# First attention of a two-layer model: own values of four heads in one group of matmuls, every second round

## The reference

```python
x = x + _L0_attn_ref(_L0_cond_ref(x, ...), ...)
x = x + _L0_ffn_ref(_L0_cond2_ref(x, ...), ...)
x = x + _L1_attn_ref(_L1_cond_ref(x, ...), ...)
x = x + _L1_ffn_ref(_L1_cond2_ref(x, ...), ...)
```

```python
def _cross_head_proj(inputs, qw1, qw2, kw1, kw2, qdd, kdd):
    h_q = jnp.einsum('bnts,btin->btsi', inputs, qw1)
    out = inputs + jnp.einsum('btsi,btin->bnts', h_q, qw2)
    h_k = jnp.einsum('bnts,bsin->btsi', inputs, kw1)
    out = out + jnp.einsum('btsi,bsin->bnts', h_k, kw2)
    out = out + inputs * jnp.transpose(qdd, (0, 2, 1))[:, :, :, None]
    out = out + inputs * jnp.transpose(kdd, (0, 2, 1))[:, :, None, :]
    return out
...
logits = _cross_head_proj(logits, pre_qw1, pre_qw2, pre_kw1, pre_kw2, pre_qdd, pre_kdd)
mask = jnp.tril(jnp.ones((t, t), dtype=bool))
logits = jnp.where(mask, logits, jnp.finfo(jnp.float32).min)
probs = jax.nn.softmax(logits, axis=-1)
probs = _cross_head_proj(probs, post_qw1, post_qw2, post_kw1, post_kw2, post_qdd, post_kdd)
o = jnp.einsum('bnts,bnsh->bnth', probs, v)
```

## Time and profile before

| | |
|---|---|
| median of three runs | 1061.58 us |
| the profiled execution's own time | 1062.01 us |
| its span, first to last instruction | 1060.2 us |
| mean granted TensorE clock | 0.942 |
| TensorE busy | 929.1 us (88%), 6216 matmuls |
| VectorE busy | 791.1 us (75%) |
| ScalarE busy | 575.2 us (54%) |
| GpSimd busy | 187.5 us (18%) |
| chain that ended last | PE 57%, DVE 25%, DMA 6% |

### The profile page before, as it was taken

The page is one execution under the profiler, slowest core; times in us unless marked ns, Lnnn a source line. Parts: engine busy times, 40 slices in busy tenths (PEclk is TensorE's granted clock), DMA queues, the critical chain, the costliest instruction groups (busy, mean ns, idle before and its releaser), DMA issues.

```text
span 1060.2 us, 18270 instructions
## 1 busy us (share of the span) xinstructions
PE 929.1 (88%) x6216; PEld 662.9 (63%) x6216; DVE 791.1 (75%) x2089; ACT 575.2 (54%) x1458; POOL 187.5 (18%) x168
## 2 busy tenths in 40 slices
PE   2889998999899989789999999788898998899993
PEld 2777776777677767664576666623333337788883
DVE  7579988998899889985299997567666766366664
ACT  2689568956795679541143332136474761455551
POOL 1101030103010301027434433200000005011111
PEclk9989998999899989969999999969998987799997
DMA  9999940000000000034367774515464544788773
GB/s 251 201 209 252 245 101 1 2 1 2 1 1 1 2 1 1 1 112 167 121 217 247 232 228 133 209 53 184 161 236 161 193 168 139 268 324 306 274 269 130
DMA packets 71453, 153.81 MB, mean 145 GB/s; under 512 B 11439, under 2 KB 53054, under 8 KB 67136
## 3 DMA queue, kind: packets, MB, share of 16 engines
q1 hardware_dynamic: 65696, 139.93, 43.5%
q0 software_dynamic: 5664, 12.71, 3.3%
HBM read 122.09 MB, written 62.19 MB: 174 GB/s over the span
## 4 chain that ended last, share of the span: by engine, by line
PE 57%; DVE 25%; DMA 6%; issue 5%; ACT 4%; POOL 3%; SPq 1%; DVEq 0%; POOLq 0%; ACTq 0%
PE ps L1785 53%; DVE arena L1191 2%; DVE arena L1535 2%; DVE den L1033 2%; DMA arena<-slots 2%; DMA arena<-split 2%; DVE arena L1174 2%; DMA made<-arena 2%; POOL slots L580 1%; POOL arena L542 1%; DVE arena L1764 1%; DVE den L986 1%; DVE arena L1217 1%; DVE backd L992 1%; DVE arena L1448 1%
## 5 line engine op out<-in xcount | busy, mean ns | idle before, releaser
L1785 PE MATMUL ps<-arena 128*128 128x128 f32 (+16 forms) x4652 | 723.6, 333 | 39.4 <-DVE arena L1191 19.1
L1785 PEld LDWEIGHTS ps<-arena 128*128 128x128 f32 (+7 forms) x4652 | 493.1, 149 | 197.7 <-issue 94.2
L1535 DVE TENSOR_REDUCE arena<-ps 128x4 f16<-128x1024 f32 (+1 forms) x48 | 58.8, 1227 | 52.4 <-PE ps L1785 52.4
L1217 DVE SCALAR_TENSOR_TENSOR arena<-arena 128x128 f32<-128x128 f32 x240 | 84.0, 410 | 0.5
L657 ACT ACTIVATE arena<-ident,arena 128x128 f32<-128x128 f32 x256 | 80.2, 390 | 0.0
L1762 DVE CAST arena<-arena 128x128 f16<-128x128 f32 (+1 forms) x128 | 33.3, 260 | 62.6 <-ACT arena L912 60.1
L817 ACT ACTIVATE arena<-ps 128x1024 f32<-128x1024 f32 x48 | 49.2, 1024 | 45.6 <-PE ps L1785 45.6
L1191 DVE SCALAR_TENSOR_TENSOR arena<-arena,ps 128x128 f32<-128x128 f32 (+1 forms) x128 | 47.2, 410 | 35.7 <-PE ps L1785 32.3
L912 ACT ACTIVATE arena<-ps,arena 128x128 f32<-128x128 f32 (+1 forms) x128 | 50.0, 416 | 43.7 <-PE ps L1785 38.7
L560 POOL DMA_INDIRECT made<-arena x47 | 53.0, 1128 | 85.6 <-DVE arena L1448 84.1
L528 POOL TENSOR_TENSOR den<-den,backd 128x512 f32<-128x512 f32 x8 | 10.5, 1309 | 277.8 <-DVE euv L1014 277.8
(11 more groups left out here) (301 smaller groups left out, 1237.1 us busy)
## 6 DMA issues: line engine op xcount, KB each, us to landing
arena<-split SPq DMA_DIRECT2D x15, 2048.0 KB, 9.3
arena<-in_w0all SPq DMA_DIRECT2D x32, 608.0 KB, 4.9
slots<-in_blank SPq DMA_DIRECT2D x17, 1040.0 KB, 18.6
arena<-in_w1all SPq DMA_DIRECT2D x16, 1024.0 KB, 6.9
split<-arena SPq DMA_DIRECT2D x32, 512.0 KB, 3.7
slots<-in_blank SPq DMA_DIRECT2D x10, 1044.0 KB, 22.9
arena<-slots SPq DMA_DIRECT2D x47, 130.0 KB, 3.2
side<-made SPq DMA_DIRECT2D x8, 512.0 KB, 5.8
```

Of the source, the lines that this page charges most:

```text
L1217: ins = dve.scalar_tensor_tensor(dst, prob[:, n % 3, tiles[tt]], w, dst, ALU.mult, ALU.add)
L1535: dve.tensor_reduce(out, ps[:, at:at + 2].rearrange("p j (r s) -> p j r s", r=nr), X, ALU.max, negate=True).then_inc(max1_done, 1)
L1785: return pe.matmul(o, l, r, start=start, stop=stop, skip_group_check=shared)
```

## The change

The own values of a pair are no longer issued in each round. In `values(p)` with odd p the own values of the four heads 2p-2 to 2p+1 are issued together, first all four heads for s = 0 and then all four for s = 1; in `values(p)` with even p none is issued. The four outputs lie on partitions 0, 32, 64 and 96. The folded matmuls stay where they were. Since the turned probabilities of a pair are now read one round later, `probT` has four buffers instead of two. `turn_out` waits for the heads of the four before it. The scratch tiles behind `probT` in the arena move by 768 words, and the arena's size is the same.

```diff
-        logit, prob, probT = cut(2, 384), cut(3, 384), cut(2, 384)
+        logit, prob, probT = cut(2, 384), cut(3, 384), cut(4, 384)
...
                 def turn_out(n):
                     act.wait_ge(t_ready, b * N0 + n + 1)
-                    if n >= 2:
-                        act.wait_ge(pv_done, b * N0 + n - 1)
-                    act.activation(probT[:, n % 2], ps[:, 2 + n % 2, 0:384], ACT.Copy).then_inc(t_read, 1)
+                    if n >= 4:
+                        act.wait_ge(pv_done, b * N0 + n // 4 * 4 - 1)
+                    act.activation(probT[:, n % 4], ps[:, 2 + n % 2, 0:384], ACT.Copy).then_inc(t_read, 1)
...
                     for s in range(TT):
-                        for n in pair:
+                        for n in range(2 * p - 2, 2 * p + 2) if p % 2 else ():
                             at = n // 4 % 2 * T
                             o = ps[32 * (n % 4):32 * (n % 4) + 32, 4 + n // 8, at + s * P:at + T]
-                            mm(o, vals[:, s, n], probT[:, n % 2, 2 * s * P:(2 + s) * P], s == 0, s == 1, True)
+                            mm(o, vals[:, s, n], probT[:, n % 4, 2 * s * P:(2 + s) * P], s == 0, s == 1, True)
                     for n in pair:
                         pe.wait_ge(folded_ready, b * N0 + n + 1)
-                        pT = probT[:, n % 2]
+                        pT = probT[:, n % 4]
```

## The result

| | before | after |
|---|---|---|
| median | 1061.03 us (7 runs, 1058.53 to 1062.09) | 1052.77 us (7 runs, 1050.32 to 1056.04) |
| profiled execution: own time, span | 1062.01, 1060.2 | 1053.66, 1051.9 |
| TensorE busy, VectorE busy | 929.1, 791.1 | 910.1, 791.7 |

The ratio is 0.9919, with a 95% interval from 0.9896 to 0.9942. The medians are 8.3 us apart; the ratio, taken of the median before, makes it 8.6 us, with an interval from 6.2 to 11.0. So the kernel is faster by some 8.5 us. 1051.2 had been forecast, inside a range from 1047 to 1058.

The account below looks back on a forecast made before the run. TensorE was taken as the bound, by half a microsecond only. Gains 3.9 + 1.0 + 4.3 + 1.9 = 11.1 us, less 0.7 for larger groups, net 10.4; 1062.0 - 10.4 = 1051.6, less 0.4: 1051.2 us, range 1047 to 1058.

Parts of the forecast that it names:

- `values(0)`: Round losing its own values, where VectorE and ScalarE had waited for TensorE: all 0.97 us gained per batch, 3.9 us.
- The group of four: Own values of four heads issued together on TensorE: 0.05 us more than a pair, fifteen groups, 0.7 us lost.
- `values(2)`: Round losing its own values: 0.5 us gained in batches 0 and 3, nothing in 1 and 2, 1.0 us together.
- `values(4)`: Round losing its own values, `fold_values` ending earlier: 1.14 us gained in two batches, 0.99 in batches 1 and 2, 4.3 together.
- Rival (a): Behind `values(4)`, `fold_values` can't get between GpSimd's sums, so nothing is gained there: 1055.5 us; chance 0.20.
- `values(6)`: Round losing its own values: saving lost in batches 0 and 3, 0.97 us gained in batches 1 and 2, 1.9 together.
- ScalarE: In short rounds TensorE will wait some 0.6 us for ScalarE between two transposes, costed at nothing.
- The cover: `scores` waits for `first_rank` anyway, hiding ScalarE's wait; if that fails, 0.42 us in each of six rounds, 2.5 us.
- the round behind `values(0)`: Sign in the new trace: rounds alternate near 8.4 us and, behind `values(0)`, 7.4 at full clock.
- the wait before `scores` behind `values(2)`: Sign in the new trace: it grows to some 0.7 us in batches 0 and 3 and 1.2 in batches 1 and 2.
- The clock: Each batch's stretch at 1.2 GHz: no change taken, some 2 us kept both ways; as rival, 1055.2 or 1047, chance 0.10.

Follow-up runs that it names:

- the buffers alone: Kernel before with four buffers of turned probabilities and the moved tiles, own values still issued in pairs every round: 1060.68 us, ratio 0.9994.
- the third session: Last of three sessions, each on another chip, its kernels sharing runs of the kernel before; the kernel after measured 1052.82 us there, ratio 0.9934.
- two column groups: Kernel after with the four heads' outputs on two of four column groups, half the heads' own values overwritten: 1060.1 us, ratio 1.0002.
- the normalisations first: Kernel after with both `normalise` of a pair ahead of `diagonals_pre` on ScalarE: 1060.89 us, ratio 0.9868, and 1049.3 us, ratio 0.9902.
- the sums made small: GpSimd's sums inside the loop cover one column of each tile: kernel after 1050.22 us, ratio 0.9895; kernel before 1058.72 us, ratio 0.998.

## Why the prediction was right, and where not

The sum was 10.4 us of gain; the result is 8.3 by the medians and 8.6 by the ratio, and the rounds give 8.6 too. Scores(3) to (7) gain 1.62 us in batches 0 and 3 and 1.21 in 1 and 2, 5.66 in all; from scores(7) to the tail 0.37 and 0.36 are lost and twice 0.07 gained, -0.6; `values(0)` brings 0.86 and 0.96 in batches 1 and 3, and 0.81 in batch 0 (scores(1) to (3), where the stretch at 1.2 GHz begins at 58.0 and 58.2: 18.62 us with the buffers alone, 17.81 in the kernel after of the third session). With 0.9 for batch 2, an estimate from the other three, that is 3.5. Together 8.6. The interval of the ratio is 2.4 us wide to either side, so that the two agree to a tenth is luck.

**The group of four: right.** First own value to the folded matmuls takes 0.787 us, against 0.775 for the pair by the same reading. I had taken 0.05 more; it is 0.01 to 0.02, and 15 groups cost 0.2 us instead of 0.7. The 1.42 us of two column groups show the other end. The Trainium skill (TensorE: Matmul & The Clock Gate, Measured speedup vs the span model) gives 3.07x for four row groups and 2.38x for three column groups, less than full speed. For four column groups of 32 in float32 these traces disagree with such a loss: it is 0.012 us over the pair.

**`values(0)`: 3.9 forecast, 3.5 found.** Nearly all comes through where VectorE and ScalarE had waited for 3 us.

**`values(2)`: 1.0 forecast, 1.2 found.** 0.51 in batches 0 and 3, 0.1 in 1 and 2. That VectorE holds batches 1 and 2 was read rightly: they stay at 8.28 whatever was done to ScalarE or the sums. In batches 0 and 3 the 0.5 came true by luck: VectorE would have let 0.70 through (8.38 to 7.68 with the normalisations first), and ScalarE, which the forecast had at nothing, took 0.19 of it.

**`values(4)`: 4.3 forecast, 4.6 found** (4 x 1.14), and `fold_values` takes 1.19 us where "near 1.2" was forecast. Rival (a) is out: it does get in between the sums, in all four batches.

**`values(6)`: 1.9 forecast, -0.6 found. This step failed.** "ScalarE is early, and the later wait for `turn_out` (0.63) is itself started by TensorE" left out that VectorE moves up against GpSimd's sums, which do not move. The step looked at the first two sums, where the move helps, and not at the last two, where `mix` now stands. The four sums cost VectorE 2.96 us instead of 2.25, and scores(7) to turn(12) grows from 7.32 to 7.89. With the sums made small in both kernels, batches 1 and 2 gain 0.95 from scores(7) to the tail (19.92 to 18.97), the 0.97 that was forecast, and batch 3 gains nothing (18.25 and 18.26), as forecast too. The Trainium skill (SBUF — State Buffer, Who interferes with whom) says that a VectorE instruction with two inputs in SBUF contends with a GpSimd instruction that reads SBUF, that the ports they share are an exclusive lock, and that one with at most one input in SBUF doesn't contend outside the modes that use both ports. The trace agrees: two pieces of `mix` end only 0.15 and 0.28 us behind the ends of GpSimd's third and fourth sum, while `first_rank`, which reads one of its two inputs from PSUM, takes 0.72 beside the second sum, as everywhere.

**ScalarE: "nothing" was too little.** The cover, `first_rank`, ends only 0.1 to 0.2 us ahead of what ScalarE releases. Its second `normalise` holds the short rounds behind `values(2)` in batches 0 and 3 and behind `values(4)` in all four, worth 0.19 and 0.09 while something else stands behind it and 0.46 (7.86 to 7.40) in the round behind `values(4)` when the sums are gone too. The forecast's price if the cover fails, 0.42 a round, is about that. Two of the forecast's own signs failed for this reason. At full clock the round behind `values(0)` is 7.97 us in batch 0, not 7.4, with 0.65 of waiting for ScalarE in it. And the wait before `scores` behind `values(2)` is 0.34 in batch 1 and gone in batch 0, not 1.2 and 0.7, since a wait of 0.54 for ScalarE now stands in front of it.

**The clock.** No change was taken, with 2 us both ways. In the profile after, batch 0 has no stretch at 1.2 GHz and batch 2 a longer one (10.2 us). That moves a single profile by 1 to 3 us in either direction: scores(1) to (3) of batch 0 is 15.12 us without the stretch and 17.81 with it (third session). Over the runs of the third session the mean granted clock is 0.946 for the kernel before and for the kernel after, so the clock doesn't carry the gain there.

So the forecast was near for a mostly right reason. The terms `values(2)`, `values(4)` and the larger groups came out 1.0 us better than forecast together; `values(0)` was 0.4 and `values(6)` 2.5 too large. The errors went both ways, and that the total is off by only some 2 us is in part luck.

## What to carry to other kernels

When an engine is shortened by a share that brings it level with two others, name what each of them does in the round, up to the end of the stage, and not only at the place where the wait was. An engine that starts by a signal that doesn't move (here GpSimd's sums) meets other instructions of its neighbour after the change: list those too. Here an experiment that reordered matmuls didn't take their overlap away; one that made them share a column group did. When a round gets shorter, read the next one too: with the normalisations first, batch 0's gave back 0.76 of 1.16 us.

## What the runs showed of the hardware

Matmuls of 32 columns on four different column groups run side by side at almost no cost (0.787 us against 0.775 for two), also if one pair is issued wholly behind the other: the second pair starts 0.027 us behind the first, while the first's own second pass starts 0.24 us behind it. Two heads on one column group run in turn (1.42 us). GpSimd's additions of 128x512 (1.3 us alone) lengthen VectorE's operations with two SBUF inputs, one piece of `mix` from 0.34 to 1.36 us; four pieces of 1.40 became 3.42 and 4.77. A lengthened operation ends a fixed time behind the end of a sum (0.15 us for 128 columns, 0.28 for 256). Operations that read one input from PSUM are not lengthened (0.72 to 0.74 us beside a sum and without one).
